# The input gate's second pass moved ahead of the eight transposes of the up product

## The reference

```python
xn = _layernorm(x)
# attention branch
x  = xn @ up_w.T                                  # "up product", 512 wide
final_gate = xn @ gate_w.T
shift = silu(causal_conv4(x) + conv_b)
q, k  = shift @ q_w.T, shift @ k_w.T
v     = sigmoid(x @ ig_w1.T @ ig_w2.T + ig_b2) * x   # the input gate
g_gate = softplus(shift @ g_w.T + g_b)
tau    = sigmoid(shift @ tau_w.T + tau_b)
...                                               # chunked scan, rms norm, down product
# feed-forward branch
h = silu(xn @ w1.T * s1) * (xn @ w2.T * s2)       # "first layer", 1024 wide
h = gelu(h @ h1.T * sh1); h = gelu(h @ h2.T * sh2)
out = x_in + attention + h @ w3.T * s3
```

## Time and profile before

| | |
|---|---|
| time, median of 3 runs | 1940.59 us (1940.5 to 1941.85) |
| the profiled execution's own time | 1940.21 us |
| its span in the trace | 1938.4 us |
| TensorE matmuls busy | 1921.8 us, 99% of the span |
| VectorE busy | 1584.1 us, 82% |
| ScalarE busy | 1295.3 us, 67% |
| granted TensorE clock, mean | 0.998 |

### The profile page before, as it was taken

One profiled execution on the slowest core, in us unless ns is written; L12 is line 12 of the kernel. 1 busy time (PEld: TensorE's weight loads), 2 busy tenths in 40 slices (PEclk: granted clock), 3 DMA queues, 4 the chain that ended last, 5 costly groups with the idle time before them and its releaser, 6 DMA issues.

```text
span 1938.4 us, 46120 instructions
## 1 busy us (share of the span) xinstructions
PE 1921.8 (99%) x16804; PEld 1902.9 (98%) x16804; DVE 1584.1 (82%) x4304; ACT 1295.3 (67%) x2687; POOL 81.2 (4%) x136
## 2 busy tenths in 40 slices
PE   8999999999999999999999999999999999999998
PEld 7999999999999999999999999999999999999998
DVE  7788888888788887888888788787888878888887
ACT  5666667767676766666766667675667666667575
POOL 0000000000000000000000000000000000000000
PEclk9999999999999999999999999999999999999999
DMA  8000000000000000000000000000000000000000
GB/s 309 7 12 13 12 2 12 12 12 12 13 1 12 13 12 12 8 5 13 12 13 12 7 6 12 13 12 13 1 12 13 12 12 12 1 13 12 13 7 8
DMA packets 23538, 34.19 MB, mean 18 GB/s; under 512 B 3170, under 2 KB 19810, under 8 KB 23364
## 3 DMA queue, kind: packets, MB, share of 16 engines
q1 hardware_dynamic: 23364, 31.43, 4.8%
HBM read 23.04 MB, written 8.39 MB: 16 GB/s over the span
## 4 chain that ended last, share of the span: by engine, by line
PE 94%; issue 2%; ACT 1%; DVE 1%; SPq 1%; DMA 0%; POOLq 0%; POOL 0%; DVEq 0%; ACTq 0%
PE fb L383 64%; PE ab L383 21%; PE ab L593 2%; PE ab L628 1%; PE ab L529 1%; PE ab L453 1%; PE ab L518 1%; PE ab L583 1%; PE fb L678 1%; SPq L289 0%; PE ab L590 0%; PE ab L469 0%; PE ab L606 0%; ACT wwhole L726 0%; DMA sgate<-stage_w 0%
## 5 line engine op out<-in xcount | busy, mean ns | idle before, releaser
L383 PE MATMUL fb<-hid1h,wwhole 128*128 128x256 f32 x2048 | 474.2, 279 | 0.1
L383 PE MATMUL fb<-hid1l,wwhole 128*128 128x256 f32 x2048 | 467.9, 276 | 0.0
L383 PE MATMUL fb<-hid0l,wwhole 128*128 128x256 f32 x2048 | 465.9, 276 | 0.0
L383 PE MATMUL fb<-hid0h,wwhole 128*128 128x256 f32 x2048 | 465.8, 276 | 0.0
L383 PEld LDWEIGHTS fb<-hid1h,wwhole 128*128 128x128 f32 x2048 | 384.5, 188 | 4.0 <-ACT raw L838 0.3
L383 PEld LDWEIGHTS fb<-hid1l,wwhole 128*128 128x128 f32 x2048 | 384.7, 188 | 0.0
L383 PEld LDWEIGHTS fb<-hid0h,wwhole 128*128 128x128 f32 x2048 | 384.5, 188 | 0.0
L383 PEld LDWEIGHTS fb<-hid0l,wwhole 128*128 128x128 f32 x2048 | 384.4, 188 | 0.0
L838 ACT ACTIVATE raw<-fb,sh_s 128x256 f32<-128x256 f32 x512 | 212.3, 465 | 150.3 <-PE fb L383 142.7
L383 PE MATMUL fb<-xntl,wwhole 128*128 128x256 f32 x1024 | 237.5, 276 | 0.0
L383 PE MATMUL fb<-xnth,wwhole 128*128 128x256 f32 x1024 | 237.5, 276 | 0.0
(11 more groups left out here) (234 smaller groups left out, 4481.6 us busy)
## 6 DMA issues: line engine op xcount, KB each, us to landing
xin<-x SPq DMA_DIRECT2D x32, 256.0 KB, 2.7
out<-xin SPq DMA_DIRECT2D x32, 256.0 KB, 2.2
stage_more<-stage_w SPq DMA_DIRECT2D x6, 512.0 KB, 7.1
sgate<-stage_w SPq DMA_DIRECT2D x4, 512.0 KB, 4.4
shift<-stage_w SPq DMA_DIRECT2D x4, 512.0 KB, 5.0
v<-stage_w SPq DMA_DIRECT2D x4, 512.0 KB, 5.6
raw<-stage_w SPq DMA_DIRECT2D x3, 512.0 KB, 6.0
mixed<-stage_w SPq DMA_DIRECT2D x3, 512.0 KB, 8.2
```

Of the source, the lines that this page charges most:

```text
L383: mm = pe.matmul(o, a, b, start=start and i == 0, stop=stop and i == len(pairs) - 1)
```

## The change

`input_gate(1)` is called right behind block 7 of the first layer, ahead of the loop with the eight transposes, and no longer behind it. Its instruction and its waits stay what they are, and nothing changes on other engines.

```diff
                     layer1(m)
+                input_gate(1)
 
                 for c in range(NC):
                     pe.wait_ge(x_ev.sem, x_ev.at(me))
                     for d in range(DB):
                         mm = pe.transpose(ab[c][:, d * P:(d + 1) * P], xbuf[:, d, W - 1 + c * CH:W - 1 + (c + 1) * CH], ident_s[:])
                     mm.then_inc(xt_mm.sem, 1)
-                input_gate(1)
```

## The result

The changed kernel takes 1958.96 us (median of 4 runs, 1958.16 to 1959.83) against 1940.55 us before (4 runs, 1939.81 to 1941.85). The ratio is 1.0096, with a 95% interval of 1.0082 to 1.011: 18.4 us or 0.95% slower, where 5.7 us was forecast. The span of the profiled execution grew from 1938.4 to 1957.9 us, by 19.5 us.

What follows compares the result with a forecast made beforehand. TensorE's instruction list was taken to bound the kernel. The seams counted as nothing and the new wait as 16 x 0.15 + 15 x 0.22 = 5.7 us, so 1940.6 + 5.7 = 1946.3 us, range 1943.4 to 1948.0.

Steps and rivals of the forecast that it cites:

- What bounds the kernel, and no wait to win: TensorE's matmuls, busy 99% of the span, set the time; no wait named in the 32 rounds, so none to end.
- The bank isn't free yet: Behind block 7, line 767 frees the pass's bank too late: 0.13 us (p = 1) or 0.20 (p = 0) after its last matmul starts.
- both rivals with no loss: Loss paid once as the wait wears off, 1940.8 us, chance 0.04; or TensorE passes the held load, 1940.6, chance 0.06.
- the short lag: Rival: the held pass streams 0.03 us after its load, so the loss is 4.2 us, 1944.8 us; chance 0.08.
- The size of the wait: At the held pass, 0.05 us release plus 0.08 lag: 0.15 us lost with p = 1, 0.22 with p = 0; 5.7 us.
- The seams: Block 7's last matmul to the projections' second: 1.35 us before, 1.34 after; taken as nothing, +-0.6 us in all.
- What the change costs without a wait: Same matmuls in another order on TensorE, so only distances at three seams can differ; taken as nothing, +-0.6 us.
- Is the loss covered anywhere: Behind the held load, no later TensorE wait shrinks, earlier results win nothing, and the loss doesn't wear off between rounds.
- more than the sum: Rival: load lag 0.11 and semaphore 0.03 us longer at the held pass, 7.6 us, so 1948.2 us; chance 0.06.

Runs made afterwards that it cites:

- The pair of runs with a filler: New order with ScalarE's early gate read, plus one redundant matmul of 384 or 512 columns ahead of the pass: 1946.13 and 1946.98 us.
- the run with the pass in the middle: Against the kernel before, the input gate's second pass put between the two groups of four transposes, with no gate wait: 1948.52 us, ratio 1.0041.
- the one with the early read and the old order: The kernel before with only ScalarE's read of the gate product's second half moved earlier, TensorE's order unchanged: 1940.66 us, ratio 1.0005.

## Why the prediction was wrong

**What bounds the kernel, and no wait to win.** Right. TensorE's list sets the time, and every microsecond came from distances between its matmuls.

**The bank isn't free yet.** Right, in both kinds of round and for the stated reason; in the first round, for which no wait was forecast, there was none. Line 767 ended about where it had, 0.14 us behind the start of block 7's last matmul with p = 1 and 0.21 with p = 0, where 0.13 and 0.20 were reckoned with. The wait didn't wear off, and nothing overtook the held load, so both rivals with no loss were wrong, and so was the short lag.

**The size of the wait.** 5.7 us forecast, 6.8 and 6.5 measured in the two traces. The mis-sized term is the lag from the load to a streaming matmul: 31 x 0.02 = 0.6 of the 1.1 us, and most of the rest is the bank that came free 0.01 us later. The lag was taken as 0.08, half of what was read at the low clock; the pass's 0.50 in place of 0.40 puts it at 0.10, near the end of 0.11 read from the hidden product at 909.13. To halve a lag measured at the low clock was less good than the row at the full clock. The new distances say the same: 1.52 to 1.54 with p = 1 (forecast 1.50) and about 1.60 with p = 0 (forecast 1.57).

**The seams.** Right: 43.2 us with the new order against 43.1 without, when no wait is in it.

**The step that failed** is the one under "What the change costs without a wait": that what can differ are "the distances at three seams". The sum ended with the second matmul of the projections and took it for granted that the 150 matmuls behind it go at 0.11 us each. They went at 0.118 in 18 rounds: 150 x 4.5 ns = 0.67 us a round, three times the wait that was being priced to the hundredth. With the two slow second hidden products that is 12.7 us, which the sum put at nothing; without it the change would have cost 5.7 + 1.1 = 6.8 us. It is also why "Is the loss covered anywhere" didn't find it: the question was only whether the loss would shrink. The rival "more than the sum" asked for a longer wait, not for another pace. The trace of before had a sign, the last 86 matmuls at 118 ns and the preparation at about the same pace, in places that one doesn't read when 32 equal rounds carry the total.

**What stays open.** Which part of the array, the load path or the list of instructions holds the two paces apart, and why 500 and 504 ns go with one and 497 to 499 and 505 with the other. How a data transfer or the reading of instructions bears on it was not tested. Not tried: other widths than 384 and 512 ahead of the pass, and other columns than 256 in the row. The pair of runs with a filler shows no slow row without a wait, but the run with the pass in the middle and the one with the early read and the old order do, so "wait and order together" is what made the projections slow in this change, not a rule.

## What to carry to other kernels

On an engine that is busy all the time, a wait of 0.2 us can cost several times its length. Here 6.8 us of waits came with 12.7 us more, because a long row of equal matmuls kept the pace that it had in its first three or four. So, where a change touches what stands ahead of such a row, count matmuls in windows of equal length behind it, round by round, and not only the gap itself; the busy share and the clock show nothing.

And before an instruction is moved ahead of others, look at who frees what it writes. Here the cheap cure was on the other side: ScalarE had an idle time in which it could free the bank 3 us earlier, and with that the same new order cost nothing.

## What the runs showed of the hardware

Rows of 256-column matmuls, each with its own load of 128 columns, ran at one of two paces at the same full clock, 113.3 or 117.8 ns, and kept it for up to 150 matmuls. The slow one shows in each matmul's duration as well, 281 ns and not 276, and in the loads: in the slow window of the trace of after every third weight load is recorded with 192 ns, in the fast one all have 187 or 188. What these two windows of after hold of `hid0h`, the fast one first (durations in ns, least, median, largest):

```profile
L383 PE MATMUL fb<-hid0h,wwhole x46: 276/276/276, 603.8 to 614.0; 128*128 128x256 f32 x46
...
L383 PEld LDWEIGHTS fb<-hid0h,wwhole x45: 187/188/188, 603.9 to 613.9; 128*128 128x128 f32 x45
...
L383 PE MATMUL fb<-hid0h,wwhole x44: 281/281/281, 721.8 to 731.9; 128*128 128x256 f32 x44
...
L383 PEld LDWEIGHTS fb<-hid0h,wwhole x43: 187/188/192, 721.9 to 731.8; 128*128 128x128 f32 x43
```

A held weight load started 0.04 us behind its semaphore, some 0.05 us behind the end of the releasing instruction, and the pass behind it carried 0.10 us more in its duration. Two executions of one kernel differed in which rounds were slow. That may be why four runs of one kernel with waits ahead of such rows spread over 6.9 us (1956.47 to 1963.33), where 20 runs of the kernel before spread over 4.1 us (1938.98 to 1943.06).
